# A two-layer transformer on one core: score, probability and projection tiles share seven PSUM banks, and the score maxima are packed and partly moved to GpSimd

## The chip, the cores and the metric

The kernel runs on one core of a Trainium2 chip. The metric is the device time of one execution in microseconds. Three runs of the kernel before took 3277.61, 3288.05 and 3293.05 us; their median is 3288.05 us. One further execution was profiled: 3268.96 us, of which the traced span is 3267.1 us.

## The reference

Eight sequences of 1024 tokens of width 256 go through two blocks. Cut to its core:

```
x = x + attention0(layernorm(x))        # 16 heads of 16, causal softmax
x = x + cp_mumoe(layernorm(x))          # entmax gates, 1024 hidden, exact gelu
x = x + attention1(layernorm(x))        # low-rank q, k, v; rotary halves of q and k; causal softmax
x = x + (sq_relu(x' @ Ws1) @ Ws2 + routed)   # x' = layernorm(x)
```

The part that matters here is causal attention: for every head, scores q k^T / 4, the maximum of each query's row over the keys it may see, exponentials of the scores less that maximum, their sum, and the product with the values.

## The kernel before, in words

**Units.** Attention of a sequence b, a layer l and a half c of its queries (512 queries each) is a pass, and a pass has four units, of four heads each: 128 units in all (`UNITS`). With c = 0 a unit sees 512 keys, with c = 1 it sees 1024.

**One unit on the engines.** Query and key are split in three bf16 parts that are stacked along the contraction, 112 rows, and loaded from DRAM by six DMAs into one of three buffers (`load_stack`, `stk_q`, `stk_k`). TensorE first computes scores with queries on the partitions (`score`, L1049): for query tile i of 128 rows and head h, a tile of up to 512 keys. A tile that ends on the diagonal is 128, 256, 384 or 512 columns wide (`score_parts`). VectorE takes its row maximum (`maximum`): for a diagonal tile with a custom operation that adds a mask while it reduces (L1599, followed by an accumulator read), for a full one with a plain reduction (L1602). When all the unit's tiles are done, VectorE forms the negative maximum and splits it in three bf16 parts with five small dependent operations (`split_max`, L1607 to L1611). TensorE transposes the parts (`max_rows`, L1055), VectorE copies them to `mT` (L1619), and a DMA of 12 KB writes them as three more rows of `stk_q`. Then TensorE computes the scores a second time, transposed, with the maxima subtracted by those three rows (`scores_t`, L1066); ScalarE takes the exponentials into `probs` (`exponentials`, L1369); GpSimd zeroes the triangle above the diagonal in 128 columns (`causal`, L1527); TensorE multiplies by the values, four heads at a time in four column groups (`weigh_values`, L1083); ScalarE copies the result out, TensorE transposes it (`normalise`, L1091) and VectorE divides.

**The other work.** Beside it run, for other sequences, the norms, projections of q, k (L1016) and v (L1024), the splitting in parts (`rest` L1513 and `part2` L1518 on GpSimd), in layer 1 the rotation: cosine product on GpSimd (L1504), pair swap and sine product on VectorE (L1583, L1585), and their sum on VectorE (`rotate`, L1591); then output projections and the two feed-forward blocks (L1150 and L1155 with gelu at L1384).

**The order.** Every engine runs its own instructions in the order of one list, `ORDER`, that `program_order` writes before the program is built. It simulates the engines with costs from `TIMES`, keeps four chains of projection and feed-forward work beside the attention, and gives TensorE at each step the ready piece of the best rank (`RANK`). DMAs are issued by SP in the same order.

**PSUM.** Banks 0 to 2 are a ring for scores, transposed maxima and normalisations, with one pair of semaphores (`s_full`, `s_drained`); banks 3 and 4 alternate for transposed scores (`st_full`, `exp_done`); bank 5 holds the attention output; banks 6 and 7 alternate for all else (`plan_tiles`). The accumulator z of the first feed-forward block holds one of the last two while hidden tiles use the other.

Of the kernel before, what the change touches and what calls it, by code (L numbers as in the profile page):

```python
# [10 lines left out]
P = 128  # L11
# [34 lines left out]
S_BANKS = (0, 1, 2)  # L46
ST_BANKS = (3, 4)
O_BANK = 5
X_BANKS = (6, 7)
LAG = 2  # L50
# [6 lines left out]
SETUP_COPIES = (11, 10)  # L57

# [97 lines left out]
def loaded(b, c):  # L156
# [23 lines left out]
TILES = ("xt", "yt", "qk_", "v_", "ao_", "logit_", "at", "g", "h1_", "hid", "fo", "route_", "up_", "down")  # L180


def score_items(u):
    b, l, g, c = UNITS[u]
    return [("s", u, i, h, p) for i in reversed(range(TPC * c, TPC * (c + 1))) for h in range(HG) for p, _ in score_parts(i)]
# [27 lines left out]
class Plan:  # L213


    def __init__(self):
        self.order, self.at = [], {}
        self.pe, self.busy = 0.0, {"ACT": 0.0, "DVE": 0.0, "POOL": 0.0, "SP": 0.0}
        self.chains, self.ready, self.locks = [[], [], [], []], [0.0] * 4, {}
        self.free, self.turn, self.ring, self.st, self.steps, self.pvs, self.held = [0.0, 0.0], 0, [], [], {}, [], []  # L220
# [30 lines left out]
    def chain_time(self, n):  # L251
        step = self.head(n)
        if step is None:
            return None
        time = self.ready[n]
        if step[0] and step[0][0][0] in TILES:
            if self.locks.get("gelu", n) != n:
                return NEVER
            time = max(time, self.free[self.turn % 2])
            if step[1] == "+gelu":  # L260
                time = max(time, *self.free)
        return time

    def give(self, n):
# [4 lines left out]
        for item in items:  # L269
# [6 lines left out]
            if item[0] in TILES:  # L276
                self.open[n] = self.turn % 2
                self.free[self.open[n]] = NEVER
                if item[0] != "hid":
                    self.turn += 1  # L280
            for engine, length in rest:
                time = self.on(engine, time, length)
            if item[0] == "z":
                if item[3] == OC - 1:
                    time = self.free[1 - self.turn % 2] = self.on("DVE", time, 0.8)
            elif pe and item[0][-1] != "_":
                self.free[self.open[n]] = time
            if item[0] == "p2":
# [15 lines left out]
    def ring_time(self):  # L304
        return self.ring[-len(S_BANKS)] if len(self.ring) >= len(S_BANKS) else 0.0

    def score_time(self):
        u = self.s_unit
        if u == len(UNITS):
            return None  # L310
        return max(self.loads[u], self.ring_time()) if u in self.loads else None

# [1585 lines left out]
```

## Time and profile before

| | |
|---|---|
| median of the runs | 3288.05 us (3277.61 to 3293.05) |
| profiled execution | 3268.96 us |
| its span | 3267.1 us |
| mean granted TensorE clock | 0.981 |
| busy, TensorE / VectorE / ScalarE / GpSimd | 2958.2 / 2447.2 / 2018.0 / 1082.0 us |
| DMA queue of SP | 264.66 MB, 34.0% of 16 engines' span |

Busy time counts an engine's instructions without overlap; a matmul's end is modelled, so that TensorE's busy time includes pipeline fill. The chain that ended last is followed back from the last instruction, at each step to what released it; time on it is time that decides the end, as far as releases are seen. A group's idle time before it is that of its own engine, and the engine after "<-" is what ended most of it.

### The profile page before, as it was taken

The page shows a single profiled execution, that of the slowest core. Times are in us where ns is not written, and L with a number is a line of the kernel's source. Part 1 is how long each engine was busy: PE and PEld are TensorE (multiplying, and loading weights), DVE is VectorE, ACT ScalarE, POOL GpSimd, SP SyncE. Part 2 cuts the span into 40 slices and gives each one's busy share as a digit, 9 for nine tenths or more (in the row PEclk, how much of TensorE's full clock was granted, in tenths as well). Part 3 has the DMA queues.
Part 4 walks back from the last instruction along what each step waited for, and adds up shares of the span by engine and source line. Part 5 has one row for each costly group of instructions (what it writes and reads, how often), then busy time and mean ns, then how long its engine had stood idle before and what let it go on. Part 6 is the DMA issues. An engine that isn't in the chain of part 4 may idle for free.

```text
span 3267.1 us, 57797 instructions
## 1 busy us (share of the span) xinstructions
PE 2958.2 (91%) x17271; PEld 1344.2 (41%) x17271; DVE 2447.2 (75%) x8243; ACT 2018.0 (62%) x4348; POOL 1082.0 (33%) x2540
## 2 busy tenths in 40 slices
PE   5788989999899989999899998999889999899896
PEld 3333443444344433434334443443444444343433
DVE  4576788859878588885878768886787848877682
ACT  3456555766567655766557665676656766566654
POOL 2314331425223351334313253232521435222411
PEclk9899999999999999999999999999999999999998
DMA  5513342335224342333514244142532434222420
GB/s 158 141 21 89 74 95 47 104 82 119 54 53 118 78 115 52 83 83 78 120 35 104 62 107 91 42 97 67 131 79 43 112 81 113 52 60 67 102 60 14
DMA packets 241216, 268.41 MB, mean 82 GB/s; under 512 B 19568, under 2 KB 208912, under 8 KB 240912
## 3 DMA queue, kind: packets, MB, share of 16 engines
q1 hardware_dynamic: 240912, 264.66, 34.0%
q8 instruction: 154, 2.52, 0.4%
q14 instruction: 150, 1.23, 0.1%
HBM read 162.35 MB, written 100.66 MB: 81 GB/s over the span
## 4 chain that ended last, share of the span: by engine, by line
PE 57%; DVE 22%; ACT 10%; issue 4%; DMA 3%; POOL 2%; SPq 2%; ACTq 0%; DVEq 0%; POOLq 0%
PE ps L1083 11%; PE ps L1066 11%; PE ps L1049 10%; PE ps L1024 6%; DVE ps L1599 6%; ACT probs L1369 5%; DVE mx L1602 4%; PE ps L1016 4%; PE ps L1155 3%; PE ps L1150 3%; ACT xn L1318 2%; PE ps L1004 2%; DMA stk_k<-k 1%; PE ps L1142 1%; PE ps L1091 1%
## 5 line engine op out<-in xcount | busy, mean ns | idle before, releaser
L1369 ACT ACTIVATE probs<-ps 128x512 f32<-128x512 f32 (+3 forms) x3072 | 1374.7, 491 | 740.6 <-PE ps L1066 718.8
L1599 DVE CUSTOM_DVE_ANT_0 ps<-ps,mask_b 128x512 f32<-128x512 f32 (+3 forms) x2048 | 978.0, 503 | 278.6 <-PE ps L1049 271.7
L1527 POOL TENSOR_SCALAR_AFFINE_SELECT probs<-probs 128x128 f32<-128x128 f32 x2048 | 599.6, 302 | 1772.4 <-ACT probs L1369 1744.3
L1066 PE MATMUL ps<-stk_q,stk_k 115*128 115x512 bf16 (+3 forms) x3072 | 876.8, 331 | 82.5 <-ACT probs L1369 52.4
L1049 PE MATMUL ps<-stk_k,stk_q 112*128 112x512 bf16 (+3 forms) x3072 | 845.0, 330 | 80.3 <-DVE mx L1599 41.0
L1602 DVE TENSOR_REDUCE mx<-ps 128x1 f32<-128x512 f32 x1024 | 702.0, 686 | 112.9 <-PE ps L1049 109.0
L1083 PE MATMUL ps<-probs,vaug 128*17 128x512 f32 (+3 forms) x6144 | 615.8, 493 | 19.4 <-POOL probs L1527 10.3
L1066 PEld LDWEIGHTS ps<-stk_q,stk_k 115*128 115x128 bf16 x3072 | 277.8, 98 | 645.3 <-ACT probs L1369 474.6
L1049 PEld LDWEIGHTS ps<-stk_k,stk_q 112*128 112x128 bf16 x3072 | 287.0, 98 | 567.9 <-issue 452.2
L1599 DVE DVE_READ_ACCUMULATOR2_ANT mx<- 128x1 f32 x2048 | 286.4, 140 | 0.0
L1016 PE MATMUL ps<-turned,wqkv 128*128 128x512 f32 x512 | 269.2, 613 | 3.1 <-ACT turned L1305 2.3
L1083 PEld LDWEIGHTS ps<-probs,vaug 128*17 128x17 f32 x6144 | 119.4, 96 | 260.4 <-issue 124.1
L1513 POOL TENSOR_TENSOR scratch<-scratch,parts 128x512 f32<-128x512 f32 x128 | 154.4, 1206 | 92.0 <-ACT scratch L1336 61.3
L1384 ACT ACTIVATE scratch<-ps 128x512 f32<-128x512 f32 x128 | 76.4, 597 | 159.1 <-PE ps L1150 158.9
L1318 ACT ACTIVATE xn<-x,shift,rstd 128x256 f32<-128x256 f32 x256 | 138.7, 598 | 56.3 <-POOL shift L1493 55.6
L1630 DVE RECIPROCAL rec<-ps 128x16 f32<-128x16 f32 x128 | 32.9, 257 | 172.4 <-PE ps L1091 162.1
L1518 POOL TENSOR_TENSOR parts<-scratch,parts 128x512 bf16<-128x512 f32 x128 | 148.6, 1162 | 39.7 <-ACT parts L1348 39.7
L1638 DVE TENSOR_TENSOR x<-ps,x 128x512 f32<-128x512 f32 x128 | 88.1, 688 | 88.3 <-PE ps L1024 87.7
L1305 ACT ACTIVATE turned<-ps 128x512 f32<-128x512 f32 x192 | 114.6, 606 | 55.0 <-PE ps L1098 34.7
L1150 PE MATMUL ps<-scratch,wout1T 128*128 128x512 f32 x256 | 133.8, 604 | 11.8 <-ACT scratch L1384 11.4
L1024 PE MATMUL ps<-wo,turned 128*128 128x256 f32 x512 | 137.6, 393 | 3.3 <-ACT turned L1305 2.8
L1024 PE MATMUL ps<-wqkv,turned 128*128 128x256 f32 x512 | 133.2, 383 | 0.0
(147 smaller groups left out, 2816.3 us busy)
## 6 DMA issues: line engine op xcount, KB each, us to landing
k<-parts SPq DMA_DIRECT2D x128, 384.0 KB, 3.6
stk_q<-q SPq DMA_DIRECT2D x256, 192.0 KB, 4.2
stk_k<-k SPq DMA_DIRECT2D x128, 384.0 KB, 6.2
q<-parts SPq DMA_DIRECT2D x64, 384.0 KB, 3.0
stk_k<-k SPq DMA_DIRECT2D x128, 192.0 KB, 4.4
x<-in_L_attn_x SPq DMA_DIRECT2D x16, 512.0 KB, 4.8
k<-parts SPq DMA_DIRECT2D x64, 128.0 KB, 3.8
stk_q<-q SPq DMA_DIRECT2D x128, 64.0 KB, 6.6
```

The lines of the kernel that those rows point to most:

```text
L1016: ins = pe.matmul(pt, wqkv[l][:, kd, D * w + P * m:D * w + P * (m + 1)], xT(2 * l, b, c, kd), start=kd == 0, stop=kd == KD - 1)
L1024: ins = pe.matmul(pt[:, D * i:D * (i + 1)], left(kd)[:, cols], right(kd), start=kd == 0, stop=kd == n_k - 1)
L1049: pe.matmul(out, q, stk_k[0:ROWS_S, slot, h, BANK * p:BANK * p + width], start=True, stop=True).then_inc(s_full, 1)
L1066: pe.matmul(st_bank[n % len(ST_BANKS)][:, cols], stk_k[0:ROWS, slot, h, P * j:P * (j + 1)], stk_q[0:ROWS, slot, h, cols], start=True, stop ...
L1083: ins = pe.matmul(o_bank[32 * h:32 * h + DH + 1, cols], vaug[:, v, j % TPC, HG * g + h, :], probs[:, STEP[u, j] % PBUF, h, cols], start=j ...
L1150: pe.matmul(pt, wout1T[:, P * o:P * (o + 1)], z1, start=True, stop=True).then_inc(done, 1)
L1318: ins = act.activation(xn[:, t, :], src[:, t, :], ACT.Identity, bias=shift[:, i, t:t + 1], scale=rstd[:, i, t:t + 1])
L1369: act.activation(probs[:, step % PBUF, h, cols], st_bank[n % len(ST_BANKS)][:, cols], ACT.Exp, scale=SCALE)\
L1513: pool.tensor_tensor(q, q, parts[:, o % PRING, 0], ALU.subtract).then_inc(rest_ready, 1)
L1527: pool.affine_select(out=diag, in_=diag, compare_op=ALU.is_ge, fill=0.0, base=0, pattern=[[1, P]], channel_multiplier=-1).then_inc(p_ready, 1)
L1599: dve.tensor_tensor_reduce(tile, tile, mask_b[:, BANK - width:BANK], 1.0, LOWEST, ALU.add, ALU.max, top)\
L1602: dve.tensor_reduce(top, tile, AX.X, ALU.max).then_inc(s_drained, 1)
```

## The change

1. **One pool of banks.** Banks 0 to 4, 6 and 7 form `BANKS`. While it writes the order, the plan gives every tile the bank that it expects to be free first (`take`), and records bank and turn in `PLACE`. Each bank has its own pair of semaphores (`full`, `drained`); the four old ones go. At most four score tiles (`S_MOST`) and three transposed-score or gelu tiles (`ST_MOST`) are in flight. z takes one bank for its eight steps, hidden tiles take any.
2. **Packed score tiles.** Tiles of 128 columns are computed for four heads into one bank, tiles of 256 columns for two. The mask is added by one more bf16 matmul (identity times mask) over the last 128 columns of each head, and VectorE reduces the whole bank with one plain reduction to four or two maxima. Diagonal tiles of 384 and 512 columns keep the custom operation.
3. **Packed transposed scores.** The same for transposed scores: one exponential and one causal select for four heads (128 queries) or two (256).
4. **Maxima's parts on GpSimd.** For c = 1 VectorE takes the greater of two columns (`greater`); GpSimd does the four split operations (`split_max`), each waiting for the one before. The maximum is no longer negated; the constant rows of `stk_k` are -1 instead. `mx` has two buffers. The plan asks for the transposed maxima 2 us (`MARGIN`) after it expects the parts.
5. **Sum of the rotated halves on GpSimd** (`rotate`).
6. **Order.** A unit's stack is loaded once the scores have reached that unit, or earlier if no unit's maxima are on their way at that moment (`may_load`); values and normalisations are given only when what they read has been placed in the order.

Its core:

```diff
-S_BANKS = (0, 1, 2)
-ST_BANKS = (3, 4)
-X_BANKS = (6, 7)
+BANKS = (0, 1, 2, 3, 4, 6, 7)
+S_MOST, ST_MOST = 4, 3
+MARGIN = 2.0
+HOLD = 0
...
+    "most": (0.0, ("DVE", 0.19)), "mx": (0.0, ("POOL", 1.15)),
...
-    "rot": (0.0, ("DVE", 1.5), ("POOL", 1.0)), "add": (0.0, ("DVE", 0.68)), "p0": (0.0, ("ACT", 0.63)),
+    "rot": (0.0, ("DVE", 1.5), ("POOL", 1.0)), "add": (0.0, ("POOL", 1.2)), "p0": (0.0, ("ACT", 0.63)),
...
+def packed(width):
+    return {P: 4, 2 * P: 2}.get(width, 1) if PACK_S else 1
...
+    def bank_time(self):
+        return min(self.free)
+
+    def take(self, key):
+        b = self.free.index(min(self.free))
+        self.place[key] = (b, self.used[b])
+        self.used[b] += 1
+        self.free[b] = NEVER
+        return b
...
+        return u <= self.s_unit or not (self.waiting or self.chains[4] or len(self.s_items) <= HOLD)
...
-                out = ring_bank(("s", u, i, h, p))[:, 0:width]
-                q = stk_q[0:ROWS_S, slot, h, P * i - BANK * c:P * (i + 1) - BANK * c]
-                pe.matmul(out, q, stk_k[0:ROWS_S, slot, h, BANK * p:BANK * p + width], start=True, stop=True).then_inc(s_full, 1)
+                n, (out, done) = packed(width), claim(("s", u, i, h, p))
+                for a in range(n):
+                    q = stk_q[0:ROWS_S, slot, h + a, P * i - BANK * c:P * (i + 1) - BANK * c]
+                    ins = pe.matmul(out[:, width * a:width * (a + 1)], q, stk_k[0:ROWS_S, slot, h + a, BANK * p:BANK * p + width],
+                                    start=a == 0, stop=a == n - 1 and n == 1)
+                if n > 1:
+                    last = out[:, 0:n * width].rearrange("q (a w) -> q a w", a=n)[:, :, width - P:width]
+                    mask = mask_b[:, BANK - P:BANK].rearrange("q (a w) -> q a w", a=1).broadcast_to([P, n, P])
+                    ins = pe.matmul(last, ident_b[:], mask, start=False, stop=True)
+                ins.then_inc(done, 1)
...
+            def split_max(u):
+
+                c = UNITS[u][3]
+                value = mx[:, u % 2, :, :, c].rearrange("q h i -> q i h")
+                if c:
+                    pool.wait_ge(most_ready, MOST["most", u] + 1)
+                else:
+                    in_sbuf(pool, score_items(u)[-1])
+                if u:
+                    written(pool, ("mt", u - 1))
+                done(pool.tensor_copy(mparts[:, :, 0], value))
+                done(pool.tensor_tensor(low[:], value, mparts[:, :, 0], ALU.subtract))
+                done(pool.tensor_copy(mparts[:, :, 1], low[:]))
+                pool.tensor_tensor(mparts[:, :, 2], low[:], mparts[:, :, 1], ALU.subtract).then_inc(mx_ready, 1)
```

## Rows read from the trace of the kernel before

**Rows 1.** The page's first part: busy us, share of the span, instructions

```profile
PE 2958.2 (91%) x17271; PEld 1344.2 (41%) x17271; DVE 2447.2 (75%) x8243; ACT 2018.0 (62%) x4348; POOL 1082.0 (33%) x2540
```

**Rows 2.** The page's fourth part: the chain that ended last, by engine

```profile
PE 57%; DVE 22%; ACT 10%; issue 4%; DMA 3%; POOL 2%; SPq 2%; ACTq 0%; DVEq 0%; POOLq 0%
```

**Rows 3.** Groups of the page: busy us, mean ns | idle before, releaser

```profile
L1066 PE MATMUL ps<-stk_q,stk_k 115*128 115x512 bf16 (+3 forms) x3072 | 876.8, 331 | 82.5 <-ACT probs L1369 52.4
...
L1083 PE MATMUL ps<-probs,vaug 128*17 128x512 f32 (+3 forms) x6144 | 615.8, 493 | 19.4 <-POOL probs L1527 10.3
```

**Rows 4.** Chain in order of time, 1513 to 1530 us: start, us, what

```profile
1513.20 1.63 PE ps L1083 x16
...
1515.15 0.86 PE ps L1024 x4
...
1521.84 0.22 PE ps L1049
```

**Rows 5.** Four stretches: length; busy of PE, PEld, DVE, ACT, POOL; clock, DMA

```profile
750.00:800.00 50.00, 46.49 (x315) 23.08 (x312) 46.74 (x165) 32.24 (x78) 29.82 (x64) 1.00 0.55 138
1100.00:1150.00 50.00, 46.77 (x307) 24.78 (x300) 23.82 (x88) 37.53 (x87) 28.82 (x66) 1.00 0.45 119
2000.00:2050.00 50.00, 44.19 (x272) 21.65 (x264) 46.38 (x143) 25.27 (x55) 8.52 (x28) 1.00 0.29 56
2300.00:2350.00 50.00, 47.76 (x306) 26.95 (x308) 42.97 (x156) 33.98 (x80) 27.59 (x62) 1.00 0.49 124
```

**Rows 6.** TensorE's groups by line, 2000 to 2050 us, the first two

```profile
L1049 PE MATMUL ps<-stk_k,stk_q 112*128 112x512 bf16 x68 | 20.0, 342 | 2.2 <-DVE mx L1599 1.1 <-DVE mx L1602 0.8
L1066 PE MATMUL ps<-stk_q,stk_k 115*128 115x512 bf16 (+3 forms) x42 | 12.9, 336 | 1.2 <-DMA stk_q<-mT 1.0
```

**Rows 7.** VectorE's instructions in order of time, two moments: start, us, what

```profile
500.52 0.69 DVE L1602 TENSOR_REDUCE mx<-ps 128x1 f32<-128x512 f32 x1
501.13 0.42 DVE L1599 CUSTOM_DVE_ANT_0 ps<-ps,mask_b 128x256 f32<-128x256 f32 x1
...
1544.37 0.46 DVE L1599 CUSTOM_DVE_ANT_0 ps<-ps,mask_b 128x256 f32<-128x256 f32 x1
...
1544.75 0.33 DVE L1599 CUSTOM_DVE_ANT_0 ps<-ps,mask_b 128x128 f32<-128x128 f32 x1
...
1545.00 0.32 DVE L1599 CUSTOM_DVE_ANT_0 ps<-ps,mask_b 128x128 f32<-128x128 f32 x1
```

**Rows 8.** Groups by line and shape, VectorE: the rotation's sum, a part's subtraction

```profile
L1591 DVE TENSOR_TENSOR scratch<-scratch 128x512 f32<-128x512 f32 x64 | 51.8, 809 | 11.0 <-POOL scratch L1504 11.0
...
L1609 DVE TENSOR_TENSOR negr<-negm,mparts 128x16 f32<-128x16 f32 x128 | 32.9, 257 | 4.4
```

**Rows 9.** Groups by line and shape: exponentials

```profile
L1369 ACT ACTIVATE probs<-ps 128x512 f32<-128x512 f32 x1536 | 854.3, 599 | 399.7 <-PE ps L1066 391.5 <-issue 0.3
...
L1369 ACT ACTIVATE probs<-ps 128x256 f32<-128x256 f32 x512 | 178.9, 386 | 108.5 <-PE ps L1066 103.2
...
L1369 ACT ACTIVATE probs<-ps 128x128 f32<-128x128 f32 x512 | 125.4, 277 | 131.5 <-PE ps L1066 126.0
```

**Rows 10.** Groups by line, GpSimd: causal selects and a 512-column subtraction

```profile
L1527 POOL TENSOR_SCALAR_AFFINE_SELECT probs<-probs 128x128 f32<-128x128 f32 x2048 | 599.6, 302 | 1772.4 <-ACT probs L1369 1744.3
L1513 POOL TENSOR_TENSOR scratch<-scratch,parts 128x512 f32<-128x512 f32 x128 | 154.4, 1206 | 92.0 <-ACT scratch L1336 61.3 <-ACT parts L1343 30.6
```

**Rows 11.** Two lines' durations, ns: min/median/max, first and last start

```profile
L1591 DVE TENSOR_TENSOR scratch<-scratch x64: 669/686/1633, 262.4 to 3075.1; 128x512 f32<-128x512 f32 x64
...
L1609 DVE TENSOR_TENSOR negr<-negm,mparts x128: 174/176/1095, 81.7 to 3198.0; 128x16 f32<-128x16 f32 x128
```

**Rows 12.** List of waits: who waited for whom: us, times, longest

```profile
PE ps L1066 <- ACT probs L1369: 52.4, 136, 1.4
...
PE ps L1049 <- DVE mx L1599: 41.0, 95, 9.6
```

More of the change, by code:

```diff
@@ L327, in score @@
         width = dict(score_parts(i))[p]
-        self.pe = max(self.pe, self.score_time()) + width / 2400 + 0.003
-        diagonal = BANK * p + width == P * (i + 1)
-        end = self.on("DVE", self.pe + HOP, (0.2 if diagonal else 0.15) + width / 960)
+        n, diagonal = packed(width), BANK * p + width == P * (i + 1)
+        start = max(self.pe, self.score_time())
+        b = self.take(item)
+        self.pe = start + n * (width / 2400 + 0.003) + (n * P / 2400 if n > 1 else 0.0)
+        end = self.on("DVE", self.pe + HOP, (0.2 if diagonal and n == 1 else 0.15) + n * width / 960)
         self.ring.append(end)
+        self.free[b] = end
         self.put(item, end)
         if not self.s_items:
-            end = self.on("DVE", 0.0, 1.1)
-            self.put(("mx", u), end)
-            self.waiting.append((u, end))
+            self.chains[4] += [("after", item)] + ([("after", ("mt", u - 1))] if u else []) + [([("most", u)], "")] * UNITS[u][3] + [([("mx", u)], "")]
             self.s_unit += 1
@@ L343, in max_rows @@
         end = self.on("DVE", self.pe + HOP, 0.4)
+        self.free[self.take(("mt", u))] = end
         self.ring.append(end)
@@ L351, in scores_t_time @@
             return None
-        n = len(self.st)
-        time = max(self.rows[u], self.st[n - len(ST_BANKS)] if n >= len(ST_BANKS) else 0.0)
-        step = n // HG
+        time = max(self.rows[u], self.st_time())
+        step = self.stepped
         if step >= PBUF:
@@ L378, in values_time, with weighing_time @@
             return None
-        u, j = self.held[0]
-        return max(self.steps[u, j], self.out.get(u - 1, 0.0) if j == 0 else 0.0)
+        return self.weighing_time(*self.held[0])
+    def weighing_time(self, u, j):
+        b, l, g, c = UNITS[u]
+        values = [("v", b, l, j // TPC, tp) for tp in range(TPC // 2)] if g == 0 else []
+        if j == key_tiles(c)[-1] and u > 1:
+            values.append(("nm", u - 2))
+        if any(item not in self.at for item in values):
+            return None
+        return max([self.steps[u, j], self.out.get(u - 1, 0.0) if j == 0 else 0.0] + [self.at[item] for item in values])
     def pair_time(self):
@@ L385, in pair_time @@
             return None
-        return max(self.values_time(), self.steps[self.held[1]])
+        times = [self.weighing_time(*step) for step in self.held[:2]]
+        return None if None in times else max(times)
     def weigh_pair(self):
@@ L408, in normalise @@
         end = self.on("DVE", self.pe + HOP, 0.75)
+        self.free[self.take(("nm", u))] = end
         self.ring.append(end)
@@ L478, in program_order @@
             plan.pe += 18.0
+            plan.free = [min(time, plan.pe) for time in plan.free]
             for engine in ("ACT", "DVE"):
```

276 lines of the change are left out of this document (138 added, 138 removed).

## The prediction, made before the changed kernel was run

> **What bounds the kernel now.** I read the page first: TensorE is busy 91% of the span, VectorE 75%, ScalarE 62%, GpSimd 33% [rows 1]. 91% looks like a kernel bound by TensorE, but the chain that ended last puts only 57% of the span on TensorE, 22% on VectorE and 10% on ScalarE [rows 2]. The two readings are reconciled by what a matmul costs when the queue is full. The groups give the transposed-score matmuls 331 ns each at their mean width of 384 columns [rows 3]; in the chain of a dense stretch one of 512 columns takes 0.22 us, sixteen value records (two steps of four heads) 1.63 us, four fp32 256-column records 0.86 us [rows 4]. The rest is pipeline fill that shows only when TensorE stalls. So I count TensorE's work by these dense steps: 3072 transposed-score matmuls and as many score matmuls at 0.163 us on average are 1001 us; 6144 value records at 0.080 us (a step's eight share their time) are 492 us [rows 3, 4]; all remaining groups counted the same way, the fp32 projections at 0.43 us for a record of 512 columns before all, give about 1067 us. Sum 2560 us: TensorE does 0.78 us of work per us of span. Some 700 us are stalls, of which the start and the end (first 100 us and last 67 us) hold about 110.
>
> Where are the others? I counted the same work in 50 us slices against VectorE's busy time. From 2000 to 2050 us VectorE is busy 46.4 of 50 [rows 5], and TensorE's nine groups, the first two of which are in [rows 6], make 36.4 us of work: rate 0.73. From 1100 to 1150 VectorE is busy 23.8 [rows 5] and the rate is 0.91. Of the 62 slices between 100 and 3200 us, 37 have VectorE busy 40 us or more: mean 43.3 us, mean rate 0.78. The other 25 have mean rate 0.85. More than half the kernel is thus run at VectorE's pace, with three score banks as the only slack: TensorE waits for a maximum before it may write the next tile.
>
> **Narrow score tiles on VectorE.** There are 128 units; each has four 256-wide and four 128-wide diagonal tiles. The masked maximum repeats every 0.38 us at 256 columns and 0.25 us at 128 (the starts of successive rows in [rows 7]), and the plain reduction of 512 columns every 0.61 us (0.69 us long) [rows 7]. Per unit 4 x 0.38 + 4 x 0.25 = 2.52 us become three reductions of 512 columns: 1.83 us. Saved 0.69 us x 128 = 88 us. That a reduction to 4 or 2 results costs what one to 1 costs is an assumption: the bound above is 0.1 us more for each, 38 us back.
>
> **Maxima's parts.** VectorE loses five small operations in a row, about 1.1 to 1.2 us with their waits (the subtraction has a mean of 257 ns) [rows 8], and keeps one of about 0.2 us for the 64 units with two key blocks: 128 x 1.15 - 64 x 0.2 = 134 us saved. The sum of the rotated halves (L1591) goes too: 64 x 0.81 = 52 us [rows 8]. VectorE in all: 88 + 134 + 52 = 274 us of 2447, or 11%.
>
> **What is added on TensorE.** Each packed tile gets a mask matmul over 512 columns (128 tiles) or 256 columns (256 tiles): at 0.22 and 0.11 us [rows 4] that is 28 + 28 = 56 us, 2.2% of its work, all of it on the engine that sets the pace elsewhere. The number of score matmuls does not change.
>
> **ScalarE and GpSimd.** Exponentials pack too: per unit 4 x 386 + 4 x 277 = 2.65 us become 3 x 599 = 1.80 us [rows 9]; 109 us of issue, nearly nothing of it on the path because ScalarE is at 62%, and where it is late a third transposed-score bank helps more. GpSimd: the causal selects go from 16 to 11 an unit. With 302 ns for 128 columns [rows 10], of which I take about 0.17 us as fixed, a select of 512 columns is 0.7 us; bounds 0.6 and, from the 512-column two-input operation, 1.2 us [rows 10]. Saved 0.7 us per unit, 90 us. Added: 64 sums of 1.2 us = 77 us, and four small operations per unit at 0.2 us plus a wait between each, 1.1 us x 128 = 140 us. GpSimd goes from 1082 to about 1210 us: cover enough, 60% of it stays idle. The parts' latency is the same 1.1 us, but they now queue behind GpSimd's selects and residual parts, and the transposed maxima, their copy, the 12 KB row transfer and the unit's transposed scores wait for them. The plan leaves 2 us before TensorE asks; what exceeds that is in a rival. Stack loads are held back behind the maxima's transfer on SP's queue: priced at nothing between -20 us (the row transfer no longer queues behind loads) and +20 us (a load comes late).
>
> **A rule that speaks against this move.** First the rows: the two-input VectorE operations on SBUF that take 686 and 176 ns in the median reach 1633 and 1095 ns [rows 11], and their means are 809 and 257 [rows 8]; over 64 and 128 of them that is 8 + 10 us lost. The Trainium skill ("SBUF — State Buffer", section "SBUF: two separate sides") says that VectorE with two SBUF inputs and GpSimd take an exclusive lock on a shared port pair and the later one is blocked for the whole instruction; by that rule these rows are explained, and more GpSimd work would block VectorE more. But the two groups in those rows are the ones that leave VectorE. By the rule the change pays back some of these 18 us; if all of them came back on the operations that stay, the sum would be 18 us worse. It changes no term.
>
> **Seven banks in one pool.** Before, scores had three banks, transposed scores two, everything else two. TensorE's idle time before transposed scores put on ScalarE is 52.4 us, and before scores on VectorE 41.0 us in the larger of two kinds [rows 12]; the real loss is larger because a stall under 0.15 us hides in the modelled end. With four and three tiles in flight these short waits should mostly go. What a hard assignment costs is that a tile waits for its planned bank though another is free.
>
> **The sum.** Heavy slices (37): VectorE 43.3 x 0.89 = 38.5 us; at 0.9 occupancy 42.8 us. TensorE 39.1 + 0.9 of mask = 40.0 us of work at rate 0.90, which light slices show, is 44.4 us. The later one sets it: 5.6 us less each, 207 us. Light slices (25): 42.4 + 0.9 = 43.3 us of work; now 0.85, with the bank waits gone I take 0.88: 49.2 us, 20 us less in all. Start and end unchanged. 3269 (the profiled execution; span 3267) - 227 = 3042 us. The median of the runs shown, 3288, lies 19 us above the profiled one, so about 3061; I give 3065.
>
> **Rivals.** (a) The saved VectorE time is mostly not what ends a wait: only its share of the chain counts. 22% of the span is 719 us [rows 2], 11% of that 79 us, less 57% of 56 us of masks, 32: 47 us gained, 3241. For it: in the 2000 us slice most of VectorE's load is the 512-wide reduction, which the change leaves alone, and only 8% would go there. Against: pooled banks let VectorE lag longer. (b) TensorE gets to 0.93 everywhere and VectorE to 0.93, which slice by slice gives 2980 + 19 = 3000; for it the slice at 2300 us, rate 0.95 with VectorE at 43 [rows 5]. (c) Slower: the maxima's parts arrive late from GpSimd. Where projections run, GpSimd is busy 29.8 of 50 us [rows 5], in strict order behind selects that wait for ScalarE, and three operations of 1.2 us can stand ahead: 3.6 us. TensorE then stands still at the unit's transposed maxima. It turns the gain into a loss from a mean delay beyond the margin of 227 / 128 = 1.8 us; with 2.4 us it is 128 x 2.4 = 307, less 227: 3288 + 80 = 3368. Against: only about a third of the slices have such a GpSimd. (d) No change: TensorE's order is static, and a plan that is wrong by a microsecond makes each pooled tile wait for its own bank, which eats the slack: about 3280.
>
> **Chances.** Forecast (3000 to 3150) 0.52; (b) 0.13; (a) 0.18; (d) 0.07; (c) 0.10. A measurement of this kernel tells about 0.5% from no change. Faster 0.83 (forecast, (a), (b)), same 0.07, slower 0.10. The range takes the forecast, (b) down to 2950 and the better part of (a), whose own centre is 3241: 2950 to 3240, some 0.8.
>
> **What would show it.** Right: VectorE near 2170 us busy, no 128- or 256-wide custom maxima, about 384 more TensorE matmuls; VectorE's share of the chain at half or less; work rate 0.86 in the slices, no slice below 0.8. Wrong: TensorE waiting for the parts from GpSimd in the list of waits, hundreds of us before the transposed maxima; reductions of packed tiles well over 0.7 us; ScalarE taking the chain share that VectorE loses, which would leave the time near 3200.

## The result: 3191 us, less than half of the gain that was forecast

The kernel after takes 3191.4 us (median of four runs, 3183.7 to 3192.2) against 3285.6 us for the kernel before on the same chip: ratio 0.971, 95% interval 0.968 to 0.974. The gain is 94 us, or 97 against the 3288 us from which the prediction started; the forecast was 223 us (3065 us). 3191 lies inside the range of 2950 to 3240 us, near its upper end. The profiled execution took 3191.3 us with a span of 3189.6.

First the page of the kernel after: engines, chain, and the groups that answer to [rows 3, 9, 10].

```profile
PE 2925.5 (92%) x17655; PEld 1405.8 (44%) x17655; DVE 2184.4 (68%) x5939; ACT 1906.6 (60%) x3708; POOL 1149.0 (36%) x2476
...
PE 57%; DVE 21%; ACT 10%; issue 4%; POOL 3%; DMA 2%; SPq 2%; ACTq 0%; POOLq 0%; DVEq 0%
...
L1418 ACT ACTIVATE probs<-ps 128x512 f32<-128x512 f32 (+1 forms) x2432 | 1235.0, 591 | 409.9 <-PE ps L1114 402.3
L1671 DVE TENSOR_REDUCE mx<-ps 128x1 f32<-128x512 f32 (+2 forms) x1408 | 889.1, 682 | 224.8 <-PE ps L1090 147.1
...
L1114 PE MATMUL ps<-stk_q,stk_k 115*128 115x512 bf16 (+3 forms) x3072 | 753.2, 330 | 40.4 <-DMA stk_q<-mT 22.6
...
L1132 PE MATMUL ps<-probs,vaug 128*17 128x512 f32 (+3 forms) x6144 | 587.3, 490 | 11.4 <-POOL probs L1575 5.8
```

VectorE's busy time came out as worked out, 2447 to 2184 us (263 saved, 274 forecast), with 384 matmuls more; GpSimd's rose by 67 us, 1082 to 1149, where 128 were forecast. But the chain did not move: 57% TensorE and 21% VectorE, as in [rows 2]. VectorE lost 11% of its work and kept its share of what ends last.

The added operations by shape, grouped by line in the kernel after:

```profile
L1671 DVE TENSOR_REDUCE mx<-ps 128x2 f32<-128x512 f32 x256 | 167.0, 683 | 47.7 <-PE ps L1095 47.2
L1671 DVE TENSOR_REDUCE mx<-ps 128x4 f32<-128x512 f32 x128 | 87.6, 684 | 25.4 <-PE ps L1095 25.0
...
L1575 POOL TENSOR_SCALAR_AFFINE_SELECT probs<-probs 128x128 f32<-128x128 f32 x1024 | 300.2, 298 | 847.3 <-ACT probs L1418 823.8 <-PE ps L1114 0.2
...
L1575 POOL TENSOR_SCALAR_AFFINE_SELECT probs<-probs 128x256 f32<-128x256 f32 x256 | 103.8, 409 | 52.1 <-ACT probs L1418 45.7 <-PE ps L1114 0.2
...
L1575 POOL TENSOR_SCALAR_AFFINE_SELECT probs<-probs 128x512 f32<-128x512 f32 x128 | 81.2, 635 | 40.9 <-ACT probs L1418 35.8
```

A reduction to two or four maxima costs what one to one maximum costs (683, 684 and 682 ns): the assumption held. The select of 512 columns takes 635 ns; 700 were taken.

The short stalls tell where the banks mattered. Idle time of the weight load, kernel before, then kernel after:

```profile
PEld ps L1066 <- ACT probs L1369: 474.6, 1102, 1.5
```
```profile
POOL mparts L1594 <- DVE mx L1676: 342.7, 26, 32.4
...
PEld ps L1114 <- ACT probs L1418: 83.6, 250, 1.2
...
PEld ps L1132 <- POOL probs L1575: 57.0, 142, 2.2
```

Before a transposed-score tile the weight load stood 1102 times behind an exponential, 475 us in all, which in the matmuls' rows shows as 52 us only [rows 12]; in the kernel after 84 us of it are left. That is idle time of the weight load's queue, and part of it passes while TensorE still works off a matmul, so it isn't lost one for one: taking 442 us of it away was worth 84 us of the total (e5, below). The row of 342.7 us is GpSimd waiting for VectorE's maxima: the parts are never late for TensorE (0.3 us idle before L1103 in all).

And a loss that the busy times hide, a stretch of the kernel after in windows (columns as in [rows 5]), then TensorE's instruction at the stall (start, us, what, idle time before it):

```profile
1640.00:1650.00 10.00, 9.62 (x77) 3.50 (x74) 9.32 (x27) 5.95 (x14) 3.79 (x11) 1.00 0.22 45
1650.00:1655.00 5.00, 2.45 (x12) 1.11 (x12) 4.83 (x15) 0.53 (x1) 1.01 (x1) 0.82 1.03 186
1655.00:1660.00 5.00, 4.69 (x8) 1.38 (x7) 2.55 (x7) 1.27 (x3) 0.84 (x4) 0.50 0.01 3
1660.00:1665.00 5.00, 5.00 (x15) 1.88 (x13) 2.63 (x6) 1.79 (x2) 0.00 (x0) 0.65 0.01 2
1665.00:1675.00 10.00, 9.91 (x27) 4.28 (x26) 5.60 (x14) 2.98 (x5) 0.00 (x0) 1.00 0.00 0
```
```profile
1654.34 1.02 PE L1178 MATMUL ps<-ident,zu 128*16 128x128 f32 x4 [1.72 <-DVE zu L1781]
```

TensorE is busy 2.45 of 5 us, then the granted clock is 0.50 and 0.65 for ten. The same stall, 1.72 us each time, stands at 1270, 1654, 2036, 2417 and 2804 us, once in each period of some 383 us, and each time five microseconds with a granted clock of 0.50 and five with 0.68 to 0.82 follow it. Over the span the mean clock is 0.965: with two levels, (1 - clock) x 2 x span gives 223 us at half clock. The profiled execution of the kernel before had 0.981, or 124 us, but it was the fastest of its kind: the 42 executions of that kernel beside the experiments below show 0.974 to 0.980, median 0.976, or 158 us. So the kernel after spends some 60 us more at half clock, and as a microsecond at half clock does half a microsecond's work, that costs 30 us at most.

### The profile page after: what moved, and what is told of

Its sections match the earlier page's. It is cut to its first block, busy times and chain, and to the rows that moved or that the text cites. A ratio compares the mean times of both kernels' runs of the same rounds, so it can differ in the third digit from the quotient of the medians.

```text
span 3189.6 us, 55047 instructions
## 1 busy us (share of the span) xinstructions
PE 2925.5 (92%) x17655; PEld 1405.8 (44%) x17655; DVE 2184.4 (68%) x5939; ACT 1906.6 (60%) x3708; POOL 1149.0 (36%) x2476
## 4 chain that ended last, share of the span: by engine, by line
PE 57%; DVE 21%; ACT 10%; issue 4%; POOL 3%; DMA 2%; SPq 2%; ACTq 0%; POOLq 0%; DVEq 0%
PE ps L1132 11%; PE ps L1114 10%; PE ps L1090 10%; DVE mx L1671 7%; ACT probs L1418 5%; PE ps L1070 5%; PE ps L1062 4%; DVE ps L1668 4%; PE ps L1204 4%; PE ps L1199 3%; PE ps L1191 2%; ACT xn L1367 2%; PE ps L1050 2%; DMA stk_k<-k 1%; PE ps L1095 1%
## 5 line engine op out<-in xcount | busy, mean ns | idle before, releaser
L1418 ACT ACTIVATE probs<-ps 128x512 f32<-128x512 f32 (+1 forms) x2432 | 1235.0, 591 | 409.9 <-PE ps L1114 402.3
L1671 DVE TENSOR_REDUCE mx<-ps 128x1 f32<-128x512 f32 (+2 forms) x1408 | 889.1, 682 | 224.8 <-PE ps L1090 147.1
L1090 PE MATMUL ps<-stk_k,stk_q 112*128 112x512 bf16 (+3 forms) x3072 | 786.4, 333 | 60.0 <-DMA stk_k<-k 16.7
L1575 POOL TENSOR_SCALAR_AFFINE_SELECT probs<-probs 128x128 f32<-128x128 f32 (+2 forms) x1408 | 483.4, 349 | 940.3 <-ACT probs L1418 905.3
L1114 PE MATMUL ps<-stk_q,stk_k 115*128 115x512 bf16 (+3 forms) x3072 | 753.2, 330 | 40.4 <-DMA stk_q<-mT 22.6
L1668 DVE CUSTOM_DVE_ANT_0 ps<-ps,mask_b 128x512 f32<-128x512 f32 (+1 forms) x1024 | 613.3, 649 | 160.1 <-PE ps L1090 155.8
L1132 PE MATMUL ps<-probs,vaug 128*17 128x512 f32 (+3 forms) x6144 | 587.3, 490 | 11.4 <-POOL probs L1575 5.8
L1594 POOL CAST mparts<-mx 128x16 bf16<-128x16 f32 x128 | 25.9, 202 | 563.7 <-DVE mx L1676 342.7
L1425 ACT ACTIVATE oT<-ps 128x512 f32<-128x512 f32 x128 | 77.3, 604 | 151.6 <-PE ps L1132 150.9
L1668 DVE DVE_READ_ACCUMULATOR2_ANT mx<- 128x1 f32 x1024 | 143.0, 140 | 0.0
```

The lines of the kernel that those rows point to most:

```text
L1090: ins = pe.matmul(out[:, width * a:width * (a + 1)], q, stk_k[0:ROWS_S, slot, h + a, BANK * p:BANK * p + width], start=a == 0, stop=a == n ...
L1114: ins = pe.matmul(out[:, width * k:width * (k + 1)], stk_k[0:ROWS, slot, h + k, P * j:P * (j + 1)], stk_q[0:ROWS, slot, h + k, cols], star ...
L1132: ins = pe.matmul(o_bank[32 * h:32 * h + DH + 1, cols], vaug[:, v, j % TPC, HG * g + h, :], probs[:, STEP[u, j] % PBUF, h, cols], start=j ...
L1418: act.activation(probs[:, step % PBUF, h:h + k, cols], src, ACT.Exp, scale=SCALE)\
L1575: pool.affine_select(out=diag, in_=diag, compare_op=ALU.is_ge, fill=0.0, base=0, pattern=[[0, k]] * (k > 1) + [[1, P]], channel_multiplier ...
L1668: dve.tensor_tensor_reduce(tile, tile, mask_b[:, BANK - width:BANK], 1.0, LOWEST, ALU.add, ALU.max, most)\
```

## The experiments

Times are medians of 4 to 10 executions. The kernel before took 3282 to 3285 us beside each, so times compare across groups to a few us; ratios are to it. "Half clock" is worked out as above. The price of an engine's time is what the total gains for each microsecond that the engine saves.

### What a microsecond of VectorE is worth

```diff
 # e1, on the kernel after; e2 likewise on the kernel before
-dve.tensor_reduce(top, tile, AX.X, ALU.max)
+dve.tensor_reduce(top, tile[:, 0:BANK // 2], AX.X, ALU.max)     # e1: tiles of one head only
```

> The changed kernel, order and banks untouched; each plain maximum over 512 keys reads only the first 256 of them (half of those keys are left out of the maxima). 1024 reductions of 0.68 us become about 0.42 us: some 270 us less of VectorE's 2184. If VectorE still sets the pace in bunched stretches (first theory: the saved time was only partly on the path because the rest of its load is concentrated), the time falls by 90 to 150 us, to 3040 to 3100. If VectorE has become free enough and other engines, waits or the clock hold the changed kernel (rival), it falls by less than 40 us and stays above 3150.

> The kernel before with the same cut: each plain maximum reads 256 of its 512 keys, order untouched, the same 270 us of VectorE taken away. It prices a microsecond of VectorE in the kernel before. My forecast priced it at about 0.8 (227 us for 274), which would give 3070 here. If only VectorE's part of the chain counts (22% of the span, rival a), it gives 60 us, 3225. By the first theory (half of the heavy stretches at VectorE's pace) 110 to 160 us, 3130 to 3175.

Both kernels leave half of the keys out of the maxima of unmasked tiles. e1: 3105.6 us, ratio 0.946 (0.943 to 0.949) against 0.971 for the kernel after: by the ratios 81 us for 260 us of VectorE (2184 to 1925), a price of 0.31. That is just short of the theory's 90 us and far from the rival's 40. e2: 3242.7 us, ratio 0.986 (0.983 to 0.989): by the ratio 46 us (35 to 56) for 246 us (2447 to 2201), a price of 0.19 (0.14 to 0.23), nearest to rival (a)'s 60 us. Rows of its page, and one of its list of waits:

```profile
PE 2966.3 (91%) x17271; PEld 1360.2 (42%) x17271; DVE 2201.0 (68%) x8243; ACT 2016.6 (62%) x4348; POOL 1083.9 (33%) x2540
...
PE 66%; DVE 12%; ACT 11%; issue 3%; DMA 3%; POOL 2%; SPq 2%; ACTq 0%; DVEq 0%; POOLq 0%
```
```profile
PEld ps L1066 <- ACT probs L1369: 507.5, 1187, 1.5
```

VectorE's chain share fell from 22% to 12% and TensorE took it, while the stalls behind the exponential grew from 475 to 508 us. So VectorE's reductions did not set the pace of the kernel before; the sum charged four times their price. This prices the 512-column reductions, the bulk of VectorE's load. No run prices the narrow tiles or the maxima's parts by themselves in the order of the kernel before.

```diff
 # e3, on the kernel after: rotate() and split_max() move from GpSimd's loop into VectorE's
+elif kind == "add":  rotate(*key)      # dve.tensor_tensor(...)
+elif kind == "mx":   split_max(*key)   # dve.tensor_copy(...), ...
```

> The changed kernel with the maxima's split and the sum of the rotated halves issued on VectorE again, at the same places of the order. VectorE gets about 128 x 0.85 + 64 x 0.8 = 160 us back, GpSimd loses about 220 us. By my sum's price of 0.8 this costs 130 us: 3320. By the first theory, 0.4 to 0.6 of it: 3255 to 3290. If GpSimd's queue made the maxima late (rival c), it costs less than 40 us or gains.

3226.4 us, ratio 0.982 (0.979 to 0.984): 35 us more for 123 us of VectorE, a price of 0.29. The moves to GpSimd are worth 35 us in this order. The time lies in the range given for late maxima, yet the parts were not late in the kernel after (0.3 us, above): the low price alone explains it.

### What the half clock costs

```diff
 # e4, on the kernel after; e12 and e17 on the kernel of e8
 # (there also the same at eight more places, 3 to 25 products, in e12, and at one, 11, in e17)
+def fill(pt, times):
+    for _ in range(times):
+        pe.matmul(pt, ident_b[:], mask_b[:], start=True, stop=True)
 def transposed_a(b, c):
-    pe.wait_ge(a_ready, ENT["epow", b, c] + 1)
     pt, done = claim(("at", b, c))
+    fill(pt, ...)                       # e4: 7, with 6 to 10 at three more places a period; e12: 21; e17: 10
+    pe.wait_ge(a_ready, ENT["epow", b, c] + 1)
```

> The changed kernel with 6 to 10 needless 512-column matmuls (0.22 us each at full clock) issued into the claimed bank ahead of four waits per sequence in which TensorE stands still for 1.5 to 2.4 us and after which the granted clock falls to half for about 10 us. Nothing else differs. If the lost clock is what the missing gain went to (221 us at half clock against 122 before, theory two), the clock rises from 0.965 to about 0.975 or more and the time falls by 20 to 45 us, to 3145 to 3170. If the clock follows something else or its loss lies beside other waits, the time stays within 10 us of 3191 or rises by the fillers that outlast their gap.

3164.8 us, ratio 0.963 (0.960 to 0.965): 27 us faster than the kernel after for work that is thrown away. Mean clock 0.975, 158 us at half clock instead of 223. Those 65 us less are worth 32 us at most, and 27 us came back: the clock's loss is real, and small beside the 129 us that miss from the forecast.

### The pool, packing and moves under the order of the kernel before

e5 keeps the old order item by item, and assigns each tile the bank of the seven that the plan has free first. It makes the maxima's parts in the new form too, though still on VectorE, which takes 64 instructions and 21 us from it; at the prices above that is some 4 us of the total. e9 keeps banks 3 and 4 for transposed scores (and the first feed-forward's hidden tiles, which its expectation does not name). e10 adds packing, e11 the moves.

```diff
+def pooled():            # over ORDER, unchanged
+    can = [b for b in range(len(BANKS)) if closes[b] < n and free[b] < NEVER]        # e9: and (b in ST_BANKS) == own
+    b = min(can, key=lambda b: free[b])
 # e10, e11: an item for two or four heads stands where the last of them stood
+    left[key] = left.get(key, n) - 1
+    if left[key]:
+        continue
```

> The order of the kernel before, item for item, with no packing and with the maxima's parts and the rotation's sum on VectorE; only the banks differ: every tile takes, out of the seven, the one whose last reader the plan expects to be done first. Before, the transposed scores' weight loads sat idle 474.6 us behind exponentials (1102 times), in the changed kernel 83.6. Third theory, formed from that and from the low price of VectorE time (0.15 us per us in the kernel before): two banks for transposed scores held the kernel before, and pooling is the larger part of the gain: 40 to 80 us, 3205 to 3245. If banks were not what held it (the packing and the engines made the gain), it stays within 20 us of 3283.

> The kernel before, its order untouched, one head to a tile and the maxima's parts on VectorE, with every kind of tile pooled over five banks except the transposed scores, which keep their own two (banks 3 and 4). The same with all seven banks in one pool took 3200 us against 3283 for the kernel before. Theory: what the pool lifts is the limit of two tiles of transposed scores between TensorE and ScalarE (475 us of short stalls of the weight load behind the exponential in the kernel before). Then this kernel gives most of the 84 us back: 3245 to 3285 us, with those stalls above 350 us. Rival: what helps is that plain scores, products, maxima and sums share banks (a third and fourth bank for products). Then 3195 to 3215 us, though the stalls behind the exponential stay. Half of each would be about 3235 us.

> The order of the kernel before with all seven banks in one pool (3200 us) and, besides, two or four heads to a narrow tile, plain and transposed; a packed tile stands where the last of its heads stood. The maxima's parts and the rotation's sum stay on VectorE. It takes some 88 us of VectorE's time away and adds 56 us of mask products on TensorE. Theory of a low price (0.15 to 0.3 us of the total per microsecond of VectorE, as the two kernels with half a reduction showed): -13 to -26 us for VectorE, +40 to +56 for TensorE, so 3215 to 3245 us. Rival, the prediction's own price of 0.8: -70 + 56, so 3175 to 3195 us. Rival of the order: the position of the tiles matters more than their cost; then anything within 40 us of 3200 and the time at half clock moves with it.

> As the kernel with the order of before, one pool and packed tiles, and with the maxima's parts and the rotation's sum moved to GpSimd: the whole change but for the new order. It takes another 123 to 186 us from VectorE. Theory of a low price: -20 to -45 us against the run beside it, so 3180 to 3220 us: about the time of the kernel after (3191), and the new order gives nothing by itself. Rival (price 0.8): -100 to -150 us against the run beside it, at or below 3090. Rival of the order: more than 25 us away from 3191 on either side; then the order written by the planner is worth that much.

e5: 3200.2 us, ratio 0.974 (0.973 to 0.976). The pool, with no packing, no moves and the old order, gives 84 us, just over the 80 of its theory. The weight load's row behind the exponential, e5:

```profile
PEld ps L1098 <- ACT probs L1402: 32.6, 114, 1.2
```

e9: 3248.8 us, 0.990 (0.988 to 0.992), with those stalls at 446 us. So of the 84 us some 48 belong to more than two tiles of transposed scores in flight, and 36 to the other kinds' sharing. The time lies at the lower edge of its theory's range: the limit of two tiles is the larger part, not nearly all.

e10: 3271.9 us, 0.996 (0.994 to 0.997). e11: 3340.1 us, 1.018 (1.015 to 1.022). Packing cost 72 us and the moves 68 more, though VectorE fell from 2426 to 2350 and 2201 us. e10 missed all of its theories; e11 answers to the rival of the order (more than 25 us away from 3191), far beyond what its text thought of. TensorE's waits in e10, then e11:

```profile
PEld ps L1146 <- POOL probs L1589: 268.2, 323, 2.4
...
PE ps L1146 <- POOL probs L1589: 144.0, 188, 2.1
...
PE ps L1117 <- DVE mparts L1688: 35.7, 34, 10.8
```
```profile
PEld ps L1146 <- POOL probs L1589: 317.6, 328, 3.7
...
PE ps L1146 <- POOL probs L1589: 182.0, 222, 2.7
...
PE ps L1117 <- POOL mparts L1611: 42.9, 39, 11.1
```

L1146 is the product with the values, L1589 the zeroing of diagonal tiles: the idle times of both queues, which may overlap, add to 412 and 500 us, where e5 has 234 and the kernel after 63. A reading of this, which e16 below tests: a packed tile is exponentiated and zeroed for four heads in one piece, so its first head is ready when the last is, and in e11 GpSimd makes the maxima's parts between. Counted on the two orders with dense costs per column, TensorE has 1.8 us of other work between the scores of a 128-wide diagonal step and its product with the values in the order before, 4.2 us in the order after; between a unit's last score and its transposed maxima 2.3 and 6.2 us.

### The other way round: parts taken out of the order of the kernel after

```diff
 # e13: each packed item becomes its two or four single ones, in the same place; e14: own banks; e15: both, and e3's edit
+for k in range(n):
+    out.append((*item[:3], item[3] + k, *item[4:]))
+def own(kind):
+    return (3, 4) if kind == "st" else (0, 1, 2) if kind in ("s", "mt", "nm", "flag") else (6, 7)
```

> The kernel after, its order kept item by item, each packed tile split again into its two or four tiles of one head, one after the other where the packed one stood; one pool of seven banks, parts and rotation sum on GpSimd. It gives VectorE and ScalarE back the fixed costs and takes the mask products off. A plan made anew without packing took 3278 us. Theory of the order (what that plan lost lay in its order, packing itself is worth little at the low price of VectorE's time, and costs 56 us of products): 3175 to 3215 us. Rival (packing carries the change): above 3250 us.

> The kernel after, its order kept item by item, but with the banks of the kernel before: three for plain scores, maxima and outputs, two for transposed scores, two for the rest. Theory (the pool is worth what it was worth under the order of before, 84 us): 3250 to 3300 us, with short stalls of the weight load behind the exponential of 350 us and more. Rival (the new order matters and the pool was only the planner's leave to make it): 3190 to 3230 us.

> Only the order of the kernel after on the kernel before: one head to a tile, three, two and two banks, maxima's parts and rotation sum on VectorE. In that order TensorE has 3 to 4 us of other work between a diagonal tile of transposed scores and the product with the values (1.8 to 2.2 us before), and 6.2 us between a unit's last score and its maxima (2.3 us before). If the order is good by itself and the banks add about 84 us: 3230 to 3290 us (no better than before, since the order was planned for a pool). If the order is what the gain is made of: at or below 3200 us. If it only fits the pool and packed tiles: over 3300 us.

e13: 3453.3 us, 1.053 (1.050 to 1.056). e14: 3753.8 us, 1.143 (1.140 to 1.146). e15, the new order alone: 4350.4 us, 1.325 (1.322 to 1.328). e13 answers to its rival (above 3250) and e15 to its last clause (over 3300), both by far more than their texts thought of; e14 lies beyond all of its own. e13 also gives VectorE back 98 us of work, some 30 of its 262 us at a price of 0.3. The rows of e14, then e15:

```profile
PEld ps L1150 <- ACT probs L1454: 636.3, 984, 2.6
...
PE ps L1150 <- ACT probs L1454: 249.9, 481, 2.1
...
PE ps L1126 <- DVE mx L1704: 112.3, 143, 2.9
```
```profile
PEld ps L1172 <- ACT probs L1476: 833.7, 1487, 2.4
...
PE ps L1172 <- ACT probs L1476: 356.7, 836, 1.9
...
PE ps L1148 <- DVE mx L1742: 211.4, 380, 2.8
```

The plan of the new order lets four score tiles and three transposed ones be in flight. With three and two banks, or with four tiles where one packed tile stood (e13: 243 and 87 us idle behind the exponential), TensorE stands behind ScalarE and VectorE tile by tile. The granted clock falls too: mean 0.950 and 0.893 in e14 and e15, or 375 and 933 us at half clock. VectorE is busy only 58% and 56% there: neither kernel lacks VectorE time.

### Is it the distance to the product with the values?

```diff
 # e16, on the kernel of e11: pv and the copy of its sums stand LAG = 2.0 us of TensorE's work later
+if item[0] == "pv":
+    held.append((time + LAG, [item]))
```

> The whole change under the order of the kernel before took 3340 us, with 500 us of short and long stalls of TensorE (weight load 318, products 182) ahead of the products with the values, behind GpSimd's zeroing of the diagonal tiles. Here those products (and the copies of their sums behind them) stand 2 us of TensorE's work later, never past the score tile that needs their buffer; the mean distance from score to product grows from 1.8 to 2.3 us to 3.7 to 5.3 us (3.0 to 4.2 in the kernel after). Theory (order of before leaves no room for a GpSimd that zeroes four heads at once and makes the maxima's parts between): stalls behind the zeroing under 120 us and the total 3210 to 3270 us. Rival (the loss of 68 us by the moves to GpSimd comes from the maxima's longer way, which this doesn't touch): 3310 to 3350 us.

3469.2 us, 1.058 (1.055 to 1.060): slower by 129 us, where the theory had it faster and the rival unchanged; neither held. Its waits:

```profile
PE ps L1200 <- ACT oT L1485: 141.9, 127, 4.2
...
PE ps L1163 <- POOL mparts L1657: 126.6, 81, 11.1
...
PEld ps L1192 <- POOL probs L1635: 43.4, 97, 1.0
```

The stalls behind the zeroing went as foreseen (500 to 44 us), and others came in their place: the transposes of the sums (L1200) now follow the copy too closely, and the transposed maxima wait for their parts. One distance mended by hand breaks the next; which of them cost the 72 and the 68 us under the old order stays open.

### Planned anew

e6 gives the planner back 3, 2 and 2 banks (`own`, used by `take` and `bank_time`), e7 sets `PACK_S, PACK_T = False, False`, e8 `S_MOST, ST_MOST = 3, 3`, e18 `MARGIN = 2.1`. In each the planner writes a new order.

> The changed kernel with the banks divided as before: three for scores, two for transposed scores, two for the rest, the order planned anew for them; packing and the moves to GpSimd stay. If pooling is the larger part of the gain, most of it goes: 3250 to 3290. If packing and the moves make the gain, 3190 to 3230.

> The changed kernel with the packing of scores and transposed scores off, order planned anew: seven banks and the moves to GpSimd stay. VectorE has 88 us more by my count, TensorE 56 us less. By the price that the half-width runs gave to VectorE's time (0.15 to 0.31) the packing is worth 13 to 27 us there and costs up to 0.6 x 56 = 34 us on TensorE: the time stays within 25 us of 3191. By my forecast's price of 0.8 it rises by 40 us or more, over 3230.

> The changed kernel with at most three score tiles in flight instead of four, transposed scores still three; order planned anew. If the depth of the score ring matters by itself, the time rises by 10 us or more. If the time is set by where a newly planned order happens to put TensorE's long stalls (theory two), it can move 20 us or more either way, together with the time at half clock.

> The kernel after, planned anew with one constant of the planner 5% larger: a unit's maxima are taken for ready 2.1 us, not 2.0 us, after their parts (this shifts the place of 5644 of 8514 steps and changes nothing else: no cost, no bank, no engine). It shows how far two plans of the same kernel lie apart. Theory (plans scatter by tens of us, and part of any difference between planned kernels is luck): 15 to 60 us away from 3191 us, on either side. Rival (the planner's orders are alike in time, and the differences seen are those of the resources): within 10 us of 3191.

e6: 3261.5 us, 0.993 (0.991 to 0.995), stalls behind the exponential 384 us: banks are worth 70 us planned anew, 562 in a fixed order. e7: 3278.4 us, 0.998 (0.997 to 0.999), 308 us at half clock: packing 87 us, against 262 in a fixed order. Its theory, from the low price of VectorE's time, had allowed 25 us at most, so what packing gives here is for the most part not VectorE time; up to 43 of the 87 us is the clock (85 us more at half clock). e8: 3149.0 us, 0.959 (0.957 to 0.960), faster than the kernel after by 42 us with fewer tiles allowed in flight. e18: 3216.8 us, 0.979 (0.975 to 0.982): 25 us slower for a constant 5% larger, with no resource changed. So at least 25 us of a difference between two planned kernels may be luck of the plan. This is one sample: how far plans can lie apart stays open. The 87 and 70 us are well beyond it, the 42 us not clearly.

> The kernel after with up to three tiles of each kind of scores in the pool (3149 us), with throwaway products of 512 columns ahead of TensorE's long waits: 19 to 21 of them in the 4.9 us wait for entmax's last values once in each sequence, and 3 to 25 ahead of eight others. They write a bank that the real product then overwrites and fill 95% of a wait. In that kernel the clock is granted at half for 238 us, some 15 us of it behind each of the seven waits of 4.9 us. Theory (a stall costs its length and then half speed for a while): 7 x 7 us and a few more come back, 3085 to 3115 us, time at half clock 110 to 150 us. Rival (VectorE or the chain of entmax sets the pace there, so that a faster clock only lengthens later waits): 3140 to 3155 us. If the products end later than the wait did, up to 10 us longer.

> The kernel after with up to three tiles of each kind of scores (3149 us), with ten throwaway products of 512 columns (2.2 us at full clock) ahead of entmax's transposes once in each sequence, and 11 ahead of one early wait. With 21 of them TensorE first waited 2.8 us for the bank and the products then ended 2.4 us after the wait that they were to fill; that gave 7 us in all. Theory (the overrun of 2.4 us ate half of what the clock gave back): ten of them fit behind the bank's wait and give 10 to 25 us more: 3115 to 3140 us. Rival (TensorE's clock behind this stall isn't what the sequence waits for): 3140 to 3155 us, no better than with 21.

e12: 3142.1 us, 0.957 (0.955 to 0.959). Half clock falls from 239 to 176 us, for 7 us that the intervals do not tell from none. TensorE in order of time at the stall, e8 and then e12:

```profile
1232.69 1.03 PE L1090 MATMUL ps<-stk_k,stk_q 112*128 112x512 bf16 x4
1238.59 1.02 PE L1178 MATMUL ps<-ident,zu 128*16 128x128 f32 x4 [4.88 <-DVE zu L1781]
...
1240.49 3.78 PE L1184 MATMUL ps<-scratch,c 16*128 16x512 f32 x4
```
```profile
1227.35 1.03 PE L1097 MATMUL ps<-stk_k,stk_q 112*128 112x512 bf16 x4
1231.19 6.17 PE L1050 MATMUL ps<-mask_b,ident_b 128*128 128x512 bf16 x20 [2.82 <-DVE mx L1680]
1237.20 0.60 PE L1187 MATMUL ps<-ident,zu 128*16 128x128 f32 x4
...
1238.53 1.98 PE L1193 MATMUL ps<-scratch,c 16*128 16x512 f32 x4 [0.20 <-ACT scratch L1492]
```

The four gates' products take 1.98 us instead of 3.78 at half clock, but the bank claimed early is 2.82 us late, the throwaway products last 6.17 us, and the transposes start 9.85 us after the row above instead of 5.90. The twenty themselves run partly at half clock (0.68 from 1230 to 1235 us, full from there on). e17, with ten of them, has the transposes 5.93 us after it and a full clock from 1225 to 1245 us. It takes 3129.6 us, 0.953 (0.951 to 0.956): 19 us better than e8, 62 better than the kernel after, and the fastest here.

## Why the prediction was off, step by step

- **VectorE's saving (274 us): right**, 263 measured. So were the mask products (work by dense steps 2560 to 2614 us, 56 forecast), packed reductions, and GpSimd's cover.
- **"More than half the kernel is thus run at VectorE's pace": the step that failed.** High busy share and low work rate stood together in 37 slices, and I took the one for the cause of the other. Saving 246 us in the kernel before was worth 46 (e2); the sum charged 207 us for 274, a price of 0.76. It got there by the line "TensorE ... at rate 0.90, which light slices show": relieved of VectorE, the heavy slices were to rise from 0.78 to 0.90. But the light slices' mean was 0.85, as the prediction itself says; 0.90 was that of the best among them. Counted in slices again from 100 to 3100 us, with the dense steps of [rows 4], the kernel after has 18 slices of 60 with VectorE at 40 us or more, and the other 42 show a mean rate of 0.84, the same as the light ones before in this count. Where VectorE is light TensorE works at 0.84, not 0.90: something else holds it there. With 0.85 in both kinds of slices the sum would have given about 85 us (37 x 2.9 less 25 x 0.9), close to the 94 measured, but by luck: it knows nothing of the pool. Why VectorE's high busy share and the low rate stood together isn't shown; both may come from phases in which every tile waits for an evacuation of its own. A chain share over a busy share, 719 / 2447 = 0.29 [rows 1, 2], was the better price; that was rival (a), and 0.19 and 0.31 lie on both sides of it.
- **The pool: undersized.** It got a share of the light slices' 20 us; alone it is worth 84 (e5). I had written that short stalls hide in the modelled end, but did not look at the weight load's own idle time, where 475 us stood.
- **Clock.** The sum had no term for it. The kernel after spends some 60 us more at half clock than most executions of the kernel before, worth 30 us at most. It isn't the new order alone: with the whole change under the old order (e11) the clock is 0.958 to 0.967, with the pool alone (e5) 0.975 to 0.979.
- **Rival (a)**, 3241, had the right mechanism for VectorE and lacked the pool; 3241 less the pool's 84 is 3157, with 3191 measured; the rest stays open, as these parts do not simply add. **Rival (c)**, late parts, didn't occur in the kernel after; the planner had left 6 us between. Under the old order TensorE waited 43 us for the parts from GpSimd (e11), but also 36 us for those from VectorE (e10), so that is not where the moves' 68 us went. Only in e16 is it large, 127 us. **Rival (d)** in its weak form is the scatter of e18.
- **The rule on the shared port** changed no term, as said, and no run here shows it at work. The two groups left; VectorE's product of the rotation, which stays (L1658), went from a mean of 864 to 994 ns, 8 us in all. But this mean does not follow GpSimd's load: it is 947 in e2, where GpSimd has the work of before, and 1006 in e3, where the sum and the parts are back on VectorE.

```profile
L1585 DVE TENSOR_TENSOR scratch<-scratch,sin 128x512 f32<-128x512 f32 x64 | 55.3, 864 | 2.2
```
```profile
L1658 DVE TENSOR_TENSOR scratch<-scratch,sin 128x512 f32<-128x512 f32 x64 | 63.6, 994 | 2.2
```

- **What would show it:** "chain share at half or less" was the sign that turned out wrong (21%), and the slices agree: in the kernel after the rate at 2300 to 2350 us is 0.71, where none was to be below 0.8.

What the gain is made of cannot be given as a sum. From one end it is pool -84, packing +72, moves +68, order -149; from the other the order alone costs 1066 us, and the rest repays it.

## What to carry to other kernels

Before pricing an engine's time by its busy share, price it by its share of the chain, and look at the idle time of the weight loads: here a thousand stalls of half a microsecond stood there and hardly showed in the matmuls' rows. Where the order of work is static, it fits one set of banks, latencies and engines: plan anew after each change, compare planned kernels only beyond the scatter of a plan whose constants are moved a little, and take a part's worth in a fixed order as its worth in that order only. And measure a few neighbours of the planner's constants: here one limit lowered by one and ten throwaway products gave 62 us, two thirds of what the whole change had given.

## What the runs showed of the hardware

- A stall of 1.72 us on TensorE in a thin stretch (busy 2.45 of 5 us) was followed by ten microseconds in which the granted clock averaged 0.58 (the windows above); around the five such stalls of this execution it was 0.58 to 0.66. At half speed those two windows cost 5 x 0.50 + 5 x 0.35 = 4.3 us of TensorE's work, more than twice the stall itself.
- Ahead of a stall, work thrown away is worth something if it ends with the wait: ten products gave 19 us, while 21 that outlasted it, with some at eight more places, gave 7, which the intervals do not tell from none.
- Reducing 512 PSUM columns on VectorE cost 682, 683 and 684 ns for one, two and four results.
- Causal selects on GpSimd cost 298, 409 and 635 ns at 128, 256 and 512 columns: about 0.19 us fixed and 0.87 ns a column.
